# Score matmuls of the exact attentions on 64 rows a head, two heads abreast

## The chip, the cores and the metric

One core of one Trainium2 chip. The time is that of one execution on the device in microseconds (us); a kernel's time is the median of its runs. A core has five engines with a queue each: TensorE (PE; its weight loads are listed apart as PEld), VectorE (DVE), ScalarE (ACT), GpSimd (POOL), and SyncE (SP), which here only issues DMAs. Each works through its own list of instructions in order, and they meet at semaphores.

## What is computed

The reference passes x, four sequences of 512 tokens by 128 features, through four layers that also read a context of 154 tokens a sequence:

- L0: cross attention with 16 heads of 8 features and a padding mask, added to x, layer norm
- L1: causal self attention, cross attention, a mixture of 8 experts (the best 2 for each token), each with a layer norm
- L2: self and cross attention with values rounded to 8 bits, and a gated feed-forward
- L3: grouped cross attention with 16 query heads of 64 features, and a gated feed-forward

The change touches the three attentions of L0 and L1 that are computed exactly:

```
scores = einsum('bqhd,bkhd->bhqk', q, k) / sqrt(8)   # + padding or causal mask
attn   = softmax(scores, axis=-1)
out    = einsum('bhqk,bkhd->bqhd', attn, v)
```

## The kernel before

Work is cut into units, one attention (or other stage) of one sequence. Units 0 to 3 are L0, 4 to 7 the causal self attention (SELF), 8 to 11 the cross attention of L1 (CROSS); these twelve are the exact units. Later stages are the experts, the 8-bit attentions, a feed-forward, the grouped attention and the last feed-forward.

**Operands.** Queries and keys are each split into three bf16 terms, whose products are summed for nearly fp32 scores. `Q_TERMS` and `K_TERMS` name eight pairs of terms, so a head of 8 features becomes a stack of 64 rows. Two heads, a pair, lie one above the other in the 128 rows of `q_stack`. The keys lie in `k_half` (`k_half_ctx` for a context), once for each head of the pair, with zeros in the 64 rows of the other head. So each score matmul runs over all 128 rows and gives one head. The stacks are made by DMA: SP writes the terms to device memory (L806) and reads them back in 16 pieces for the keys (L788) and 16 for the queries (L795).

**Scores, first way round (`scores_exact`).** A step takes one pair of heads and, in a cross unit, two query tiles of 128, in SELF one query tile n with its 128(n+1) keys. A cross unit has 16 steps, a SELF unit 32. The two heads go to the two halves (PSUM banks) of `score[at_step % 2]`. L0 adds the padding row with a second matmul for each; SELF adds the causal mask by a matmul with the identity (`ident_bf`, `causal`). DVE then takes the maximum over the keys (L1927). Two steps can be in flight.

**Scores, second way round (`scores_transposed`).** A block has keys on the 128 partitions and up to 512 queries as columns, in one bank of `trans`. Keys times queries (L1124), in SELF the mask (L1126), then minus the maxima through a matmul with `ones` (L1128). ACT takes the exponential of the whole bank (L1483). A group of 4 heads has 5 blocks in a cross unit (one a head, and a tail for the keys past 128, L1116 and L1118, which runs over all 128 rows) and 10 in SELF, with one or two pieces each. The 320 blocks of all units are the slots: PE's order is, for each slot w, block w; then the score steps that `place_steps` spreads evenly over the slots (those of the next group of heads, the first of them 3 slots ahead); then the items of `EXACT_ITEMS` (projections K, Q and V, normaliser N1 and N2, output projection W, transpositions H and "tops", and others); then, if a batch of blocks is complete, their weighing of the values (`weigh_batch`, L1149, L1151), which works on 32 columns of the array a head, four heads at a time.

```
for w in range(EXACT_SLOTS):
    scores_transposed(w)
    for u, i in steps_in_slot(w):
        scores_exact(u, i)
    for it in EXACT_ITEMS.get(w, ()):
        item(*it)
    if weigh_in_slot(w) is not None:
        weigh_batch(weigh_in_slot(w))
```

Block w waits until the exponential of block w-2 is done. The keys and queries of the next unit are projected in slots 0 and 1 of a cross unit (1 and 2 in SELF); its first score step is in slot 13 of 20, or 28 of 40, and waits for its stacks. `split_tops` on DVE splits the maxima of a group in three bf16 terms, in columns 32j to 32j+2 for head j of the group.

## Time and profile before

| | |
|---|---|
| median of 3 runs | 1636.1 us (1633.66 to 1645.17) |
| the profiled execution | 1633.61 us, span 1631.8 us |
| busy in the span | PE 1165.1, PE's weight loads 676.5, DVE 1109.7, ACT 903.4, POOL 677.9 us |
| mean granted clock of TensorE | 0.825 |

The span runs from the first to the last instruction; start and end of the program lie around it (1.8 us). Busy times are sums over stages with different limits. Matmuls are pipelined, so a matmul's own duration is longer than the time from its start to the next start. The granted clock has two levels, 1.00 (2.4 GHz) and 0.50 (1.2 GHz); a value between is a mean over time.

### The profile page before, as it was taken

The page shows a single profiled execution, that of the slowest core. Times are in us where ns is not written, and L with a number is a line of the kernel's source. Part 1 is how long each engine was busy: PE and PEld are TensorE (multiplying, and loading weights), DVE is VectorE, ACT ScalarE, POOL GpSimd, SP SyncE. Part 2 cuts the span into 40 slices and gives each one's busy share as a digit, 9 for nine tenths or more (in the row PEclk, how much of TensorE's full clock was granted, in tenths as well). Part 3 has the DMA queues.
Part 4 walks back from the last instruction along what each step waited for, and adds up shares of the span by engine and source line. Part 5 has one row for each costly group of instructions (what it writes and reads, how often), then busy time and mean ns, then how long its engine had stood idle before and what let it go on. Part 6 is the DMA issues. An engine that isn't in the chain of part 4 may idle for free.

```text
span 1631.8 us, 27753 instructions
## 1 busy us (share of the span) xinstructions
PE 1165.1 (71%) x8832; PEld 676.5 (41%) x8832; DVE 1109.7 (68%) x3127; ACT 903.4 (55%) x2546; POOL 677.9 (42%) x1048
## 2 busy tenths in 40 slices
PE   2689999999978789684435354444438778888888
PEld 1355555555544448682111111122215444553545
DVE  2466776777667756277989899977764666666533
ACT  0344455555544346347767778888882254545542
POOL 5201110110111142545888878877771245344320
PEclk9899999999989999896555555555558899999999
DMA  5322341121072211216645557665560112111000
GB/s 160 69 49 55 64 139 36 43 73 35 17 150 48 46 45 46 80 46 162 120 95 111 100 108 123 119 106 107 106 108 10 26 38 55 28 33 48 1 1 26
DMA packets 263825, 115.53 MB, mean 71 GB/s; under 512 B 215928, under 2 KB 252672, under 8 KB 261504
## 3 DMA queue, kind: packets, MB, share of 16 engines
q1 hardware_dynamic: 258720, 107.34, 31.2%
q0 software_dynamic: 2048, 4.20, 0.9%
q10 hardware_dynamic: 2912, 2.22, 0.5%
q8 instruction: 71, 1.16, 0.3%
q14 instruction: 74, 0.61, 0.1%
HBM read 38.54 MB, written 16.45 MB: 34 GB/s over the span
## 4 chain that ended last, share of the span: by engine, by line
PE 39%; POOL 19%; DVE 15%; issue 15%; ACT 8%; DMA 2%; SPq 1%; another core or an unknown queue 0%; POOLq 0%; ACTq 0%; DVEq 0%
POOL arena L2236 10%; ACT arena L1536 5%; PE acc L1151 3%; PE trans L1124 3%; PE trans L1128 3%; POOL inv_total L2225 2%; PE misc L988 2%; PE misc L994 2%; PE score L1098 2%; PE trans L1275 2%; PE score L1090 2%; DVE minus_top L1927 2%; POOL arena L2183 2%; PE score L1287 2%; PE score L1289 2%
## 5 line engine op out<-in xcount | busy, mean ns | idle before, releaser
L2236 POOL TENSOR_SCALAR arena<-arena,inv_total 128x512 f16<-128x512 f32 (+1 forms) x512 | 299.6, 585 | 57.3 <-DVE inv_total L2003 16.4
L1927 DVE TENSOR_REDUCE minus_top<-score 128x4 f32<-128x616 f32 (+4 forms) x256 | 204.2, 804 | 150.9 <-PE score L1094 61.2
L2099 POOL TENSOR_TENSOR rstd<-spread,minus_half 128x4 f32<-128x4 f32 x36 | 37.6, 1044 | 534.0 <-DVE spread L1617 464.6
L1536 ACT ACTIVATE arena<-score,minus_top,exp_scale 128x512 f32<-128x512 f32 (+1 forms) x340 | 210.4, 625 | 17.5 <-POOL arena L2236 7.5
L1483 ACT ACTIVATE arena<-trans 128x512 f32<-128x512 f32 x240 | 140.5, 597 | 119.1 <-PE trans L1128 113.3
L1574 ACT ACTIVATE arena<-arena,minus_top 128x154 f32<-128x154 f32 x256 | 105.1, 412 | 131.8 <-DVE minus_top L2068 131.7
L1232 PE MATMUL score<-arena 32*128 32x512 bf16 (+1 forms) x340 | 68.4, 455 | 144.2 <-ACT arena L1536 143.1
L2009 DVE TENSOR_REDUCE top_score<-score 128x2 f32<-128x1024 f32 (+1 forms) x128 | 135.7, 1060 | 0.6 <-PE score L1232 0.5
L2256 POOL TENSOR_TENSOR arena<-arena,inv_total 128x512 f32<-128x512 f32 x64 | 66.5, 1040 | 144.7 <-DVE inv_total L2076 130.9
L1128 PE MATMUL trans<-arena 128*128 128x512 bf16 (+3 forms) x384 | 123.3, 330 | 0.0
L1536 ACT ACTIVATE arena<-trans,minus_top,exp_scale 128x154 f32<-128x154 f32 (+1 forms) x172 | 105.5, 620 | 16.3 <-POOL arena L2236 11.7
L1090 PE MATMUL score<-arena 128*128 128x154 bf16 x512 | 74.2, 244 | 51.9 <-issue 45.8
L2063 DVE CUSTOM_DVE_ANT_0 arena<-score,arena 128x154 f32<-128x154 f32 x256 | 66.0, 314 | 60.1 <-PE score L1312 59.7
L1992 DVE TENSOR_SCALAR arena<-arena 128x1024 bf16<-128x1024 f16 x192 | 102.7, 535 | 6.0 <-DMA arena<-arena 6.0
L1232 PEld LDWEIGHTS score<-arena 32*128 32x128 bf16 x340 | 14.2, 102 | 195.1 <-ACT arena L1536 177.8
L1527 ACT ACTIVATE minus_top<-top_score,exp_scale 128x2 f32<-128x2 f32 (+1 forms) x192 | 56.4, 294 | 60.9 <-DVE top_score L2009 60.4
L1232 PE MATMUL trans<-arena 32*128 32x154 bf16 (+1 forms) x172 | 34.4, 448 | 73.3 <-ACT arena L1536 73.2
L1090 PEld LDWEIGHTS score<-arena 128*128 128x128 bf16 x512 | 49.0, 104 | 79.7 <-issue 52.4
L1151 PE MATMUL acc<-arena 128*32 128x512 f32 (+3 forms) x768 | 78.5, 496 | 2.7 <-ACT arena L1483 2.7
L1501 ACT ACTIVATE arena<-score,arena 128x128 f32<-128x128 f32 x184 | 51.9, 371 | 49.8 <-PE score L1188 42.4
L1251 PE MATMUL acc<-arena 128*32 128x128 bf16 x1536 | 58.6, 304 | 28.1 <-DVE oT L2017 15.5
L1124 PE MATMUL trans<-arena,late 128*128 128x512 bf16 (+3 forms) x256 | 77.3, 302 | 0.2 <-ACT arena L1483 0.2
(283 smaller groups left out, 3075.7 us busy)
## 6 DMA issues: line engine op xcount, KB each, us to landing
arena<-q_terms SPq DMA_DIRECT2D x176, 64.0 KB
late<-arena SPq DMA_DIRECT2D x128, 64.0 KB, 2.0
q_terms<-arena SPq DMA_DIRECT2D x36, 128.0 KB
late<-k_terms SPq DMA_DIRECT2D x64, 64.0 KB
arena<-arena SPq DMA_TRANSPOSE x192, 3.1
by_expert<-zeros SPq DMA_DIRECT2D x2, 1472.0 KB, 9.8
arena<-by_expert SPq DMA_DIRECT2D x10, 256.0 KB, 2.9
from_expert<-arena SPq DMA_DIRECT2D x10, 256.0 KB
```

Of the source, the lines that this page charges most:

```text
L1090: ins = nc.tensor.matmul(dst, q_stack[:, u % 2, c, t * P:(t + 1) * P], k_half_ctx[:, u % 2, s, c, 0:CTX], start=True, stop=(stage(u) != L0))
L1124: nc.tensor.matmul(dst, keys, q_stack[:, u % 2, h // 2, q0:TOKENS], start=True, stop=False)
L1128: ins = nc.tensor.matmul(dst, ones[:, j, :], top_rows[:, g % 2, q0:TOKENS], start=False, stop=True)
L1151: ins = nc.tensor.matmul(acc[32 * j:32 * j + 32, q0:TOKENS], v_cols[:, k, 4 * g + j, :], src, start=(b % half == 0 and k == 0), stop=(last ...
L1232: ins = nc.tensor.matmul(quant_score[i % 3][:, j, z * n:(z + 1) * n], qT_codes[r:r + 32, u % 2, t * P:(t + 1) * P], k4_codes[r:r + 32, u % ...
L1483: nc.scalar.activation(expT[w % SLOTS], trans[w % 2][:, :], ACT.Exp, bias=bias)\
L1536: ins = nc.scalar.activation(probs[:, i % 3, j, of], quant_score[i % 3][:, j, of], ACT.Exp, bias=minus_top[:, at_col:at_col + 1], scale=ex ...
L1574: ins = nc.scalar.activation(gq_exp_p[:, i % 3, h, :], shifted[:, i % 3, h, :], ACT.Exp, bias=minus_top[:, at_col:at_col + 1], accum_out=t ...
L1927: nc.vector.tensor_reduce(dst, src, axis=AX.X, op=ALU.max, negate=True).then_inc(top_ready, 1)
L1992: nc.vector.tensor_scalar(pT_codes[:, of, :, :].rearrange("p k q -> p (k q)"), pT_raised[:, of, :, :].rearrange("p k q -> p (k q)"), -HALF ...
L2009: nc.vector.tensor_reduce(of_step(top_score, i), src, axis=AX.X, op=ALU.max, negate=True).then_inc(quant_top, 1)
L2236: ins = nc.gpsimd.tensor_scalar(codes[:, (i - 1) % CODE_SOURCES, j, to], probs[:, (i - 1) % 3, j, of], inv_total[:, at_col:at_col + 1], HA ...
```

## The change

A head's score matmuls use only its own 64 rows: head s of a pair takes rows 64s to 64s+63 of `q_stack` and of a single `k_stack` without zeros. The two heads' matmuls are issued one behind the other and go to two banks. The same holds for the blocks: blocks w and w+1 are raised together, piece by piece, at the even slots; a cross unit's tail stays alone and on 128 rows. For the pairs to hold one head of either half, the last SELF blocks of a group take heads (0, 2) and (1, 3) instead of (0, 1) and (2, 3), and the maxima of head j go to row block 2(j % 2) + j // 2. Masks on 64 rows need the identity and the mask in two halves, so the causal addition becomes two matmuls a head. The constants for this (`masks`) come with the late loads and are converted on DVE in slot 14 of unit 1 (`mk`). The padding row's three terms go to rows 0 to 2 of either half, for which POOL multiplies with `term_row` and adds. The clearing of `k_half` and `k_half_ctx` on POOL is gone. The steps' places are as before.

```diff
+def transposed_with(w):
+    u, g = BLOCKS[w][:2]
+    n = (w - FIRST_SLOT[u]) % PER[u]
+    if n % 2:
+        return []
+    return [w, w + 1] if n + 1 < PER[u] else [w]
...
-    at(exact, 0, ("zk", 0))
+    at(exact, FIRST_SLOT[1] + 14, ("mk", 0))
...
-                     (causal_f, io["causal"]), (causalT_f, io["causalT"]), (head_mask[:, :], io["head_mask"]),
+                     (head_mask[:, :], io["head_mask"]), (term_row[:, :], io["term_row"]),
...
-                    for s in range(2):
-                        bank = score[at_step % 2][:, s, :]
-                        if is_cross(u):
-                            for j in range(2):
-                                t = 2 * n + j
-                                dst = bank[:, j * CTX:(j + 1) * CTX]
-                                ins = nc.tensor.matmul(dst, q_stack[:, u % 2, c, t * P:(t + 1) * P],
-                                                       k_half_ctx[:, u % 2, s, c, 0:CTX], start=True,
-                                                       stop=(stage(u) != L0))
...
+                    banks = [(half_rows(s), score[at_step % 2][:, s, :]) for s in range(2)]
+                    if is_cross(u):
+                        for j in range(2):
+                            t, of = 2 * n + j, slice(j * CTX, (j + 1) * CTX)
+                            for r, bank in banks:
+                                ins = nc.tensor.matmul(bank[:, of], q_stack[r, u % 2, c, t * P:(t + 1) * P],
+                                                       k_stack_ctx[r, u % 2, c, 0:CTX], start=True, stop=(stage(u) != L0))
+                            if stage(u) == L0:
+                                for r, bank in banks:
+                                    ins = nc.tensor.matmul(bank[:, of], ones_pad[r, :], pad_rows[r, u % 2, :],
                                                            start=False, stop=True)
+                    else:
+                        width = P * (n + 1)
+                        for r, bank in banks:
+                            nc.tensor.matmul(bank[:, 0:width], q_stack[r, u % 2, c, n * P:(n + 1) * P],
+                                             k_stack[r, u % 2, c, 0:width], start=True, stop=False)
+                        for h in range(2):
+                            for r, bank in banks:
+                                ins = nc.tensor.matmul(bank[:, width - P:width], unit_halves[r, h, :], causal[r, h, :],
+                                                       start=False, stop=(h == 1))
                     ins.then_inc(scores_ready, 1)

                 def scores_transposed(w):
+                    blocks = transposed_with(w)
+                    if not blocks:
+                        return
                     u, g, _, pieces = BLOCKS[w]
                     if w >= 2:
-                        pe.wait_ge(expT_ready, w - 1)
+                        pe.wait_ge(expT_ready, blocks[-1] - 1)
...
+                    for n in range(len(pieces)):
+                        _, k, q0, c0 = pieces[n]
+                        two = [(j, half_rows(j % 2), 2 * g + j // 2, trans[z % 2][:, c0:c0 + TOKENS - q0])
+                               for z in blocks for j in [BLOCKS[z][3][n][0]]]
+                        for j, r, c, to in two:
+                            keys = (k_stack_ctx if is_cross(u) else k_stack)[r, u % 2, c, k * P:(k + 1) * P]
+                            nc.tensor.matmul(to, keys, q_stack[r, u % 2, c, q0:TOKENS], start=True, stop=False)
                         if is_causal(u):
+                            for h in range(2):
+                                for j, r, c, to in two:
+                                    nc.tensor.matmul(to[:, 0:P], unit_halves[r, h, :], causalT[r, h, :], start=False, stop=False)
+                        for j, r, c, to in two:
+                            ins = nc.tensor.matmul(to, ones[r, j, :], top_rows[r, g % 2, q0:TOKENS], start=False, stop=True)
+                    ins.then_inc(scoresT_ready, 2)
...
+                    elif name == "mk":
+                        dve.wait_ge(late_in, 16 * LATE_LOADS)
+
+                        for h in range(2):
+                            r = slice(h * P // 2, (h + 1) * P // 2)
+                            nc.vector.tensor_scalar(before_bf[r, :], masks_f[r, 1, h, :], 0.0, None, ALU.is_lt)
+                        nc.vector.tensor_copy(masks[:, :, :, :], masks_f).then_inc(masks_ready, 1)
```

## Rows read from the trace of the kernel before

**Rows 1.** The page's 40 slices of 40.8 us: busy tenths of PE, granted clock.

```profile
PE   2689999999978789684435354444438778888888
...
PEclk9899999999989999896555555555558899999999
```

**Rows 2.** Windows by unit (2, 5, 9, 11): stretch, length, busy time of each engine, clock.

```profile
134.20:172.50 38.30, 35.66 (x262) 19.99 (x260) 28.12 (x69) 20.30 (x34) 4.64 (x7) 1.00 0.37 75
...
271.10:329.00 57.90, 55.17 (x500) 31.88 (x499) 42.83 (x90) 30.71 (x53) 4.25 (x4) 1.00 0.17 51
...
484.20:524.70 40.50, 32.62 (x203) 17.25 (x201) 28.64 (x92) 18.07 (x35) 4.61 (x7) 0.92 0.26 49
...
566.20:602.10 35.90, 28.21 (x166) 13.01 (x163) 24.61 (x87) 15.61 (x29) 19.28 (x19) 1.00 0.14 45
```

**Rows 3.** Timeline of PE at three first score steps: start, duration, work, idle time before.

```profile
122.72 0.23 PE L1090 MATMUL score<-arena 128*128 128x154 bf16 x1 [2.28 <-issue]
...
162.67 0.23 PE L1090 MATMUL score<-arena 128*128 128x154 bf16 x1 [1.05 <-issue]
...
513.31 0.42 PE L1090 MATMUL score<-arena 128*128 128x154 bf16 x2 [5.96 <-issue]
```

**Rows 4.** Timeline of SP's DMA issues in unit 9.

```profile
489.88 1.80 SPq L806 DMA_DIRECT2D q_terms<-arena  x3
...
498.05 5.37 SPq L795 DMA_DIRECT2D arena<-q_terms  x16
```

**Rows 5.** Timeline of PE around a weighing (128x128, then 128x32, then 128x128).

```profile
206.47 0.22 PE L1098 MATMUL score<-late,arena 128*128 128x128 bf16 x1
206.52 0.22 PE L1100 MATMUL score<-causal,ident_bf 128*128 128x128 bf16 x1
206.67 1.06 PE L1151 MATMUL acc<-arena 128*32 128x512 f32 x8
207.67 1.12 PE L1149 MATMUL acc<-arena 128*128 128x512 f32 x2
208.63 0.38 PE L1124 MATMUL trans<-arena 128*128 128x512 bf16 x1
208.84 0.38 PE L1128 MATMUL trans<-arena 128*128 128x512 bf16 x1
```

**Rows 6.** Timeline of PE in the grouped attention; fp32 matmuls have two records each.

```profile
1423.40 0.79 PE L1312 MATMUL score<-arena 64*128 64x154 f32 x8
1424.13 0.65 PE L1323 MATMUL trans<-ident,arena 128*128 128x128 f32 x4
```

**Rows 7.** Timeline of ACT in unit 5: two exponentials back to back.

```profile
308.43 1.09 ACT L1483 ACTIVATE arena<-trans 128x512 f32<-128x512 f32 x2
```

**Rows 8.** Windows of parts of units 0, 2, 5 and 9, columns as in rows 2.

```profile
46.50:52.10 5.60, 5.60 (x37) 4.75 (x38) 2.40 (x3) 0.97 (x2) 0.00 (x0) 0.50 0.10 33
...
134.20:139.70 5.50, 5.43 (x36) 2.66 (x34) 5.02 (x15) 3.18 (x6) 0.00 (x0) 1.00 0.11 25
163.70:172.50 8.80, 8.80 (x78) 5.49 (x77) 5.43 (x11) 5.74 (x10) 3.61 (x6) 1.00 0.40 66
...
271.10:290.70 19.60, 18.36 (x139) 9.87 (x138) 15.43 (x31) 9.88 (x18) 0.00 (x0) 1.00 0.34 97
290.70:305.90 15.20, 13.72 (x132) 8.42 (x131) 12.62 (x36) 7.45 (x13) 4.25 (x4) 1.00 0.20 68
305.90:317.50 11.60, 11.60 (x119) 6.85 (x118) 7.39 (x12) 7.02 (x13) 0.00 (x0) 1.00 0.01 1
...
513.30:516.30 3.00, 2.99 (x17) 2.17 (x18) 0.86 (x2) 1.16 (x2) 0.00 (x0) 0.50 0.00 0
...
513.30:524.70 11.40, 10.60 (x73) 6.63 (x74) 8.01 (x38) 5.42 (x11) 0.00 (x0) 0.87 0.00 0
```

**Rows 9.** Timeline of DVE in the first block: the wait for the first loads.

```profile
11.41 0.23 DVE L759 CAST ident_bf<-ident 128x128 bf16<-128x128 f32 x1 [6.98 <-DMA attn_w<-in_attn_w]
```

**Rows 10.** Timeline of POOL: the clearing of `k_half`.

```profile
32.48 6.92 POOL L2150 MEMSET late<- 128x8192 f32 x1
```

More of the change, by code:

```diff
@@ L100, in exact_batches @@
             out.append((g, [[(j, 1, P, 0), (j, 3, 3 * P, 3 * P)] for j in range(4)]))
-            out.append((g, [[(j, 2, 2 * P, 0), (j + 1, 2, 2 * P, 2 * P)] for j in (0, 2)]))
+            out.append((g, [[(j, 2, 2 * P, 0), (j + 2, 2, 2 * P, 2 * P)] for j in (0, 1)]))
     return out
@@ L395, in build @@
         ident_bf = sb("ident_bf", [P, P], bf16)
-        causalT = sb("causalT", [P, P], bf16)
-        causal = sb("causal", [P, P], bf16)
+        masks = sb("masks", [P, 3, 2, P], bf16)
+        unit_halves, causal, causalT = (masks[:, n, :, :] for n in range(3))
         q_bias = sb("q_bias", [P, 2])
         head_mask = sb("head_mask", [P, 4])
+        term_row = sb("term_row", [P, 3])
         expert_no = sb("expert_no", [P, EXPERT_BLOCKS])
@@ L1130, in scores_transposed @@
-                    ins.then_inc(scoresT_ready, 1)
+                    if len(blocks) == 1:
+                        bank = trans[w % 2]
+                        pe.wait_ge(k_tail_ready, seq(u) + 1 + (B if stage(u) == CROSS else 0))
+                        for z in range(2):
+                            nc.tensor.matmul(bank[:, :], k_tail[:, u % 2, g, z * P:(z + 1) * P],
+                                             q_stack[:, u % 2, 2 * g + z, :], start=(z == 0), stop=False)
+                        nc.tensor.matmul(bank[:, :], ones_tail, top_rows[:, g % 2, :], start=False, stop=True)\
+                            .then_inc(scoresT_ready, 1)
+                        return
```

98 lines of the change are left out of this document (37 added, 61 removed).

## The prediction

> **What bounds the kernel now.** The page's slices come first: up to slice 15 (some 600 us) PE is busy in 8 or 9 tenths and its clock is nearly full; from slice 18 to 29 the clock is at its lower level and PE is not what matters [rows 1]. All edits lie before 602 us, so only the twelve exact units count. I cut them at the start of each unit's first exponential (ACT's 320 exponentials are the 320 blocks, in order). The windows by unit [rows 2] show three kinds: an L0 unit takes 38.3 us with PE busy 35.7; a SELF unit 57.9 with PE 55.2, DVE 42.8; a CROSS unit 40.5 with PE only 32.6, DVE 28.6. CROSS has fewer matmuls than L0 and is no shorter, so PE can't be its whole bound. The waits of PE tell why: at the first score step of the next unit PE stands still 2.28, 1.05 and 5.96 us [rows 3] (a third L0 wait is 2.2, two further CROSS waits 7.5 and 4.2, unit 0 has 10.1). These are waits for that unit's query and key stacks: SP issued the query terms at 489.88, the last sixteen reads until 503.4, and PE goes on at 513.31 [rows 3, 4], 23.4 us after the first issue; in the L0 units it is 22.3. That trip is DMA, and the change issues as many DMAs of the same size. So a cross unit is a chain: slots 0 and 1 up to the query projection, the trip, then slots 13 to 19. What PE saves between the projection and slot 13 only lengthens the wait. SELF units show no such wait: their trip has 28 slots to hide in.
>
> **The price of a matmul.** From start to start in the timeline 512 columns take 0.21 to 0.22 us and 128 take 0.05 to 0.06 [rows 5]; I use 0.216 and 0.056, and 0.067 for 154, which is 0.42 ns a column and 2.5 ns for each matmul.
>
> **Two heads abreast (removed work).** No bf16 pair on 64 rows is in this trace. The nearest row is the fp32 score step of the grouped attention, the same form (64 rows each, two banks): eight records of 154 columns in 0.79 us, the next operation 0.73 after its start [rows 6]. One after another they would need 8 x 0.128 = 1.03 and a switch; two abreast 4 x 0.13 = 0.52, and 0.2 for the switch and the first weights: 0.73. So I take full overlap. Per L0 unit: 16 steps of eight matmuls become four pairs, -0.27 each, -4.3; 16 head blocks of two 512-column matmuls, -0.216 each, -3.5; sum -7.8. CROSS has no padding matmuls: -2.1 - 3.5 = -5.6. SELF: the score columns, 8 x 1280, are halved, -4.3; the causal additions double in number and go two abreast, 0; the blocks have 4 x 10,240 key and top columns, halved, -8.5; sum -12.8.
>
> **Switches of the array (added work).** Between matmuls of different row or column shape PE loses time: the 128-column matmul at 206.52 should hand over at 206.58, the 32-column ones begin at 206.67, 0.095 more; the 128x128 fp32 one at 207.67 takes 0.96 to the next start where two passes of 0.427 are 0.85, so 0.106 of weight load is exposed; bf16 weights expose about 0.01 [rows 5]. Now only the weighing of values switches: 8 times in a cross unit, 26 in SELF. Walking the slot table with the new order (64-row stretches broken by every projection, transposition of tops, normaliser, tail and weighing) gives about 33 in L0, 34 in CROSS, 47 in SELF: +3.3, +3.5 and +3.0 us. PE's own work changes by -4.5, -2.1 and -9.8 a unit, -67 us over twelve units (19 + 39 + 9). That is the most that can be won.
>
> **Blocks raised in pairs (a new wait).** The pair (w, w+1) may be raised only when the exponentials of all blocks before w are done; now block w needs only w-2. Behind the waiting PE stand the score steps, so DVE waits too. One cycle: raise 0.55 or 0.66 (1280 or 1536 columns a pair of blocks), 0.16 until the last columns are out, 0.04 to ACT, two exponentials 1.09 [rows 7], 0.05 back: 1.9 to 2.0 us. In slots 20 to 39 of a SELF unit nothing but blocks, steps and weighing runs, 11.6 us for 10 slots, PE without a gap, DVE 7.4 [rows 8]. Its five pairs will hold 1.7, 0.9, 2.0, 0.9 and 2.7 us of PE work (the raise, one or two steps of 0.17 to 0.33, in three of them a weighing of 0.5 to 0.95 and its switches), 8.2 in sum; with a floor of 1.95 each it is 10.5, and 10.8 with part of the present surplus (11.6 measured, 10.4 counted). Gain 0.8 for each of two groups, 1.6, where PE alone would give 6. In slots 0 to 19 (34.8 us, PE 32.1, DVE 28.05 [rows 8]) PE falls by 6.0 to 26.1, two short pairs give 2.3 back, 28.4; DVE is now level with it. With the present surplus of 2.7 and a little for two engines of equal load, 31.6: gain 3.2. SELF: 4.8 a unit, 19 for four. Bounds: 0 (every pair adds a stall that the surplus doesn't hold) to 9.8 (ACT runs in the shadow).
>
> **Cross units.** Slots 0 and 1 of an L0 unit: PE 5.4, DVE 5.0 of 5.5 [rows 8]; at most 0.4. Slots 13 to 19: 2.1 less PE work out of 8.8 [rows 8], some 0.5 back in the pair after each single tail, which must await the tail's exponential (N1, N2 and H stand behind three of the four tails and hide them). Gain 1.5 each. But the wait of 1.05 grows to some 3; after the waits of 2.3 the granted clock is at its lower level for 4 us, after the one of 1.05 it is not; after the CROSS wait it is 0.50 for 513.3 to 516.3 [rows 8]. One more cold stretch costs 1.5. Units 1 to 3: 3 us. CROSS 8 to 10: 0.2 + 1.1 - 0.7 = 0.5 each, DVE already 8.0 of 11.4 there [rows 8]; unit 11, which has no successor to wait for but a router chain on DVE, 1. Sum 2.5. The first scores and slots 0 and 1 of unit 0 run largely at the lower clock [rows 8], where a step of eight matmuls costs 8 x 0.128 = 1.03 and DVE's reduction of it 0.8: six to eight such steps on the path, 2 us, and slots 13 to 19, 1.5.
>
> **Edits with small prices.** The first block now loads six things instead of seven before DVE's last preparations, which wait for them [rows 9], and three DVE conversions go: an issue and a landing of 0.4 to 0.5 and 3 x 0.14, -0.9 (0.7 with what the new mask preparation takes, below). The memset of 6.9 us on POOL goes [rows 10], and nobody waited for it; POOL's padding work gains some 1.2 us a sequence, POOL being idle most of a unit. The new mask preparation (three DVE instructions, 1.1 us by the elements of the casts beside it) stands in unit 1, slot 14, just behind the wait for DMA: 0 to +1, I take 0.2. Splitting the tops keeps its four small instructions. Late loads grow by 0.4 MB; their first reader is POOL, 20 us ahead of need: 0.
>
> **The sum**: 0.7 + 3.5 + 3 + 19 + 2.5 = 28.7 us. The profiled execution took 1633.6 (span 1631.8), so 1605; the median of the three runs is 2.5 above it, so **1607**.
>
> **Rivals.** (a) *PE's saving counts in full*: ACT's cycle falls into the gaps, DVE keeps up. For: in SELF, ACT is busy only 30.7 of 57.9 [rows 2]. Against: the order of instructions ties raise and exponentials, whatever the mean. SELF 9 each, the rest 15: 1636 - 51 = 1585, at best 1569. (b) *Narrow pairs don't overlap*: two weight loads of 128 columns may not go in 0.056 us; the fp32 pair has 0.13 for them [rows 6]. Then each 128-column pair costs 0.112. A SELF unit has some 150 of them (64 in the steps, 64 in the blocks, the rest narrow keys), +8.5 us of PE work: SELF gains 0 to 1, 1636 - 10 = 1626. (c) *Slower, by the clock*: PE would stand still about 1 us in three pairs of five. If the lower level were granted in slots 20 to 39 of SELF, 8.2 us of work in 10 slots become 16.4 against 11.6 now: +9.6 a unit, 38 for four, and with the other gains of 22 the kernel takes 1652; it decides from about two thirds of those stretches upward. Against: the last CROSS unit kept 1.00 with PE busy 28.2 of 35.9 [rows 2]. (d) *The change doesn't do what it says*: pairs go one after another. SELF then adds 6.8 of causal columns and 3.0 of switches, the cross units 1 each: 1636 + 47 = 1683. It turns to a loss in SELF once a pair costs 1.5 single streams (19.6 x 1.5 + 3 = 32.4).
>
> By the Trainium skill, "TensorE: Matmul & The Clock Gate", section "Measured speedup vs the span model", four row tiles gave 3.07 times, not four; two tiles with that loss would cost 1.3 streams, SELF's work would fall by 3.9 rather than 9.8, and the result would lie at (b). The trace's pair [rows 6] shows no such loss. The same page, "A second HAM failure mode: psum-queue depth-cycling", says that short idle stretches between groups of matmuls can keep pulling the clock down, which is (c); no row here shows it for gaps of 1 us.
>
> **Chances.** Forecast 0.60, (a) 0.14, (b) 0.16, (c) 0.06, (d) 0.04. The range leaves out (c), (d) and the best of (a): 1578 to 1627. 1% (16 us) is about what a measurement can tell from no change: faster 0.75 (forecast, (a), a third of (b)), same 0.16, slower 0.09.
>
> **What will show it.** Pairs: starts of the new score matmuls a few ns apart and 0.216 us from pair to pair at 512 columns; PE work in SELF near 46 a unit. The cycle: in slots 20 to 39 PE idle ahead of the raised pairs, released by ACT, 10.5 to 11 us for 10 slots. The trip: waits before the first score step longer by about 2 us, 22 to 23 us from issue to use as before. Clock 1.00 through SELF. I am wrong if SELF stays at 57 or goes under 50, or if the cross units shrink by more than 3.

## The result, and the profile after

| | before | after |
|---|---|---|
| median of the runs measured together | 1645.01 us (18 runs, 1629.49 to 1653.57) | 1634.83 us (18 runs, 1617.46 to 1646.02) |
| ratio | | 0.9931, 95% interval 0.9903 to 0.996 |
| profiled execution, span | 1633.61, 1631.8 us | 1629.24, 1627.4 us |
| first exponential, start of unit 4, of unit 8, end of unit 11 | 42.9, 212.1, 442.6, 602.1 | 40.0, 206.0, 429.1, 594.2 |
| PE, PE's weight loads, DVE, ACT busy | 1165.1, 676.5, 1109.7, 903.4 | 1109.7, 600.2, 1109.3, 895.0 |

The ratio is of the means of the fast runs, 16 of the 18 after, and not of the two medians. Faster by 0.4 to 1.0%, some 11 us, where 29 was forecast. In the profiled executions the exact units gain 7.9: the start 2.9, units 0 to 3 went from 169.2 to 166.0, SELF from 230.5 to 223.1, and CROSS got longer, from 159.5 to 165.1. What follows unit 11 took 1024 to 1043 us in all the executions told of here, whatever the kernel, so below it is also told where unit 11 ends. That is one execution each: units 1 to 3 alone differ by up to 5.4 us between executions of the same code.

Two of the page's slice lines of after, to be held against [rows 1]:

```profile
PE   2688888787777679784435354444439787898888
...
PEclk9899999999998999796555555555559889999999
```

Up to slice 15 PE has gone from mostly 8 and 9 tenths to 7 and 8; the clock is as uneven as it was. Windows of units 2, 5, 9 and 11, as in [rows 2]:

```profile
125.60:166.40 40.80, 33.35 (x266) 14.33 (x262) 28.06 (x68) 19.76 (x34) 4.66 (x7) 0.92 0.40 80
263.20:318.90 55.70, 44.84 (x630) 23.94 (x628) 42.16 (x90) 29.35 (x53) 4.25 (x4) 1.00 0.16 53
470.40:512.70 42.30, 31.29 (x204) 12.73 (x200) 29.25 (x92) 18.18 (x36) 4.62 (x7) 0.91 0.27 50
556.40:594.20 37.80, 26.84 (x162) 9.90 (x160) 23.97 (x83) 15.45 (x29) 19.34 (x19) 0.95 0.14 43
```

In SELF PE has lost 10.3 us of work (55.17 to 44.84) and the unit 2.2 (57.9 to 55.7). Units 2 and 9 are longer with less work, at a clock of 0.92 and 0.91 that was 1.00 and 0.92. Now SELF's ten-slot stretches (slots 0 to 9, 10 to 19, 20 to 29) and the stretch of unit 9 behind the wait, as in [rows 8]:

```profile
263.20:282.80 19.60, 16.17 (x172) 7.76 (x170) 15.54 (x31) 9.52 (x17) 0.00 (x0) 1.00 0.36 115
282.80:297.30 14.50, 11.15 (x168) 6.54 (x166) 12.34 (x35) 7.22 (x14) 4.25 (x4) 1.00 0.13 46
297.30:308.10 10.80, 8.76 (x152) 4.82 (x150) 7.13 (x12) 6.59 (x13) 0.00 (x0) 1.00 0.01 2
...
499.73:512.70 12.97, 11.34 (x76) 5.15 (x76) 8.81 (x39) 5.57 (x12) 0.00 (x0) 0.76 0.00 0
```

Slots 20 to 29 are what was forecast, 10.8. Slots 0 to 9 take 19.6 as before, with PE's 18.4 down to 16.2. The stretch of unit 9 behind the wait went from 11.4 to 13.0, at a clock of 0.76 that was 0.87. PE's timeline where a pair of blocks is raised (start, duration, work):

```profile
270.52 0.34 PE L1149 MATMUL trans<-arena,late 64*128 64x384 bf16 x2
270.69 0.28 PE L1153 MATMUL trans<-masks 64*128 64x128 bf16 x4
270.80 0.33 PE L1155 MATMUL trans<-arena 64*128 64x384 bf16 x2
270.97 0.22 PE L1149 MATMUL trans<-arena,late 64*128 64x128 bf16 x2
```

Two matmuls of 384 columns take 0.17 from start to next start, four of 128 take 0.11: one after another they would take 0.33 and 0.22 (by the prediction's 0.42 ns a column and 2.5 ns for each matmul). Both kinds run fully abreast. The next timeline is cut from one of all engines, around the end of one pair and the start of the next, in slots 20 to 29:

```profile
296.85 0.38 PE L1155 MATMUL trans<-arena 64*128 64x512 bf16 x2
...
297.27 1.08 ACT L1509 ACTIVATE arena<-trans 128x512 f32<-128x512 f32 x2 [1.00 <-PE trans L1155]
...
297.71 0.64 PE L1177 MATMUL acc<-arena 128*32 128x256 f32 x8
298.40 0.10 PEld L1149 LDWEIGHTS trans<-arena,late 64*128 64x128 bf16 x2 [0.54 <-ACT arena L1509]
298.41 0.39 PE L1149 MATMUL trans<-arena,late 64*128 64x512 bf16 x2
```

ACT waits 1.00 for PE to finish the pair, then PE waits for both exponentials: the two take turns. PE's first score steps of units 2, 3 and 10 (to [rows 3]) and SP's issues in unit 9 (to [rows 4]):

```profile
114.20 0.31 PE L1106 MATMUL score<-arena 64*128 64x154 bf16 x2 [3.91 <-issue]
...
154.85 0.31 PE L1106 MATMUL score<-arena 64*128 64x154 bf16 x2 [3.68 <-issue]
...
499.73 0.44 PE L1106 MATMUL score<-arena 64*128 64x154 bf16 x4 [6.70 <-issue]
```

```profile
476.10 1.80 SPq L818 DMA_DIRECT2D q_terms<-arena  x3
...
483.95 5.33 SPq L807 DMA_DIRECT2D arena<-q_terms  x16
```

From 476.10 to 499.73 are 23.6 us: the trip is what it was (23.4), and the waits are longer (2.28, 1.05 and 5.96 before).

### The profile page after: what moved, and what is told of

The parts are those of the page before. It is cut to its first block, busy times and chain, and to the rows that moved or that the text cites. A ratio compares the mean times of both kernels' runs of the same rounds, so it can differ in the third digit from the quotient of the medians.

```text
span 1627.4 us, 28786 instructions
## 1 busy us (share of the span) xinstructions
PE 1109.7 (68%) x9344; PEld 600.2 (37%) x9344; DVE 1109.3 (68%) x3126; ACT 895.0 (55%) x2546; POOL 681.6 (42%) x1054
## 3 DMA queue, kind: packets, MB, share of 16 engines
q1 hardware_dynamic: 258720, 107.61, 31.6%
q0 software_dynamic: 2048, 4.20, 0.9%
## 4 chain that ended last, share of the span: by engine, by line
PE 35%; POOL 19%; issue 17%; DVE 15%; ACT 10%; DMA 2%; SPq 1%; POOLq 0%; another core or an unknown queue 0%; ACTq 0%; DVEq 0%
POOL arena L2268 10%; ACT arena L1562 5%; PE acc L1177 3%; PE trans L1149 2%; POOL inv_total L2257 2%; PE misc L999 2%; PE misc L1005 2%; PE trans L1301 2%; ACT arena L1509 2%; POOL arena L2215 2%; PE score L1313 2%; PE score L1315 2%; PE trans L1155 2%; PE acc L1175 1%; DVE arena L1727 1%
## 5 line engine op out<-in xcount | busy, mean ns | idle before, releaser
L1509 ACT ACTIVATE arena<-trans 128x512 f32<-128x512 f32 x240 | 134.5, 596 | 113.8 <-PE trans L1155 107.8
L1562 ACT ACTIVATE arena<-trans,minus_top,exp_scale 128x154 f32<-128x154 f32 (+1 forms) x172 | 105.6, 621 | 16.2 <-POOL arena L2268 11.8
L1106 PE MATMUL score<-arena 64*128 64x154 bf16 x512 | 45.7, 248 | 54.0 <-issue 32.7
L1509 ACT ACTIVATE arena<-trans,arena 128x512 f32<-128x512 f32 x80 | 52.3, 687 | 30.6 <-PE trans L1155 27.0
L2044 DVE TENSOR_REDUCE top_score<-trans 128x2 f32<-128x1024 f32 (+1 forms) x64 | 67.4, 1053 | 0.0
L1447 ACT COPY arena<-misc 128x512 bf16<-128x512 bf16 x48 | 28.1, 586 | 70.1 <-PE misc L989 67.3
```

The lines of the kernel that those rows point to most:

```text
L1509: nc.scalar.activation(expT[w % SLOTS], trans[w % 2][:, :], ACT.Exp, bias=bias)\
L1562: ins = nc.scalar.activation(probs[:, i % 3, j, of], quant_score[i % 3][:, j, of], ACT.Exp, bias=minus_top[:, at_col:at_col + 1], scale=ex ...
L2044: nc.vector.tensor_reduce(of_step(top_score, i), src, axis=AX.X, op=ALU.max, negate=True).then_inc(quant_top, 1)
```

## The experiments

Kernels that were measured together share their runs of the kernel before; each ratio is to those. "Ends at" is the end of unit 11 in the profiled execution (before 602.1, after 594.2). The changed kernel's own ratio, 0.9931, is from other runs than those of the experiments.

### 1. The clock behind the waits

Filler matmuls (their results are overwritten) ahead of the wait for the stacks, in the changed kernel and in the one before:

```
+ if i == 0 and u in FILL:
+     pe.wait_ge(top_ready, at_step - 1)
+     for _ in range(FILL[u]):   # after {1:24, 2:14, 3:14, 4:10, 9:28, 10:26, 11:16}, before {1:36, 2:8, 3:3, 4:8, 9:28, 10:22, 11:15}
+         nc.tensor.matmul(score[at_step % 2][:, 0, :], ident_bf[:, :], q_stack[:, (u - 1) % 2, 0, :], start=True, stop=True)
```

> The changed kernel, with filler matmuls of 512 columns (10 to 28 of them, 2 to 6 us) ahead of PE's wait for the stacks of the next cross unit, into the score bank that the next step overwrites; they change no value. Theory A (the clock): in the changed kernel the granted clock is 0.50 for 68.5 us before the end of the exact units, against 51.2 before, nearly all of it right behind these waits, which costs some 10 us. Expected: the cold stretches behind the waits go (under 30 us in all), units 1 to 3 about 1.5 and units 8 to 11 about 2 us shorter each, the kernel 8 to 12 us below the changed one (ratio to before 0.985 to 0.988). Rival B (the clock costs nothing there, since the trip of the stacks or DVE sets the end of each unit): units as long as before within 0.5, ratio 0.993 as for the changed kernel.

> Control: the kernel before, with the same filler (3 to 36 matmuls of 512 columns) in front of the same waits. Theory A: its cold stretches behind the waits are 21.6 us in all against some 43 in the changed one, so it gains about half, 3 to 6 us (ratio 0.996 to 0.998), and the distance between this and the changed kernel with filler is larger than the 11 us between the two without: 14 to 18. Rival B: ratio 1.00.

After with filler: 0.9932 (0.9903 to 0.996), ends at 589.4, clock at 0.50 for 34 us instead of 68. Before with filler: 0.9987 (0.9955 to 1.002), ends at 594.2, 14 us at 0.50. Unit 2 of the one and of the other:

```profile
124.70:162.40 37.70, 33.92 (x276) 14.37 (x272) 28.05 (x68) 19.59 (x33) 4.66 (x7) 1.00 0.38 82
```

```profile
131.50:170.40 38.90, 36.31 (x265) 20.29 (x264) 28.22 (x69) 20.28 (x34) 4.65 (x7) 1.00 0.37 75
```

Units 1 to 3 took 113.6 with filler against 120.8 without; in the kernel before 115.8 against 117.9. So in L0 the clock is where the gain went, as far as one execution each can tell, and 2.2 of the 3 us forecast appear once it is held. In CROSS the changed kernel got nothing back: 167.0 against 165.1. But there the filler didn't hold the clock: waits of 3.8 and 3.6 us were left at two trips, and 24 of the 34 us at 0.50 lie in these units (31 without filler). Where it was held better, CROSS did get shorter: in the kernel before from 159.5 to 154.6, with 3 us at 0.50 instead of 24. So this run doesn't clear the clock in CROSS.

The expectations were missed: both ratios are above theirs, and the two kernels with filler are 6.6 us apart in the median and 4.8 in where unit 11 ends, not 14 to 18. The filler is worth 5 us in the changed kernel (1623.3 against 1628.5 of the kernel with serial steps below, which does the changed kernel's work and was measured together with it; with 95% confidence that difference is known to some 4.5 us), not 8 to 12. The clock took a part of the gain, and not most of it.

### 2. One block at a time; one head after the other

First the old raising (block w after the exponential of w-2), each block on 64 rows; then the changed kernel with all of one head's score matmuls of a step before the other's.

```
- pe.wait_ge(expT_ready, blocks[-1] - 1)
+ pe.wait_ge(expT_ready, w - 1)          # and the pieces of block w alone
```
```
- for j in range(2): for r, bank in banks: ...     # and the same for keys and masks in SELF
+ for r, bank in banks: for j in range(2): ...
```

> The changed kernel with blocks raised one at a time again, each on its head's 64 rows, with the old wait (block w waits for the exponential of w-2); the score steps stay two heads abreast. PE's work in SELF goes up by 8.5 (key and top columns) and 3.6 (64 more causal additions of 0.056) a unit, to some 55. Theory A (DVE and the order of work bound slots 0 to 19, ACT's cycle slots 20 to 39, and pairing the blocks is what took 0.8 per ten slots): SELF units back at 57 to 59 us, slots 20 to 39 at 11.6 or more per ten slots, cross units 0 to 1 longer than in the changed kernel, ratio to before 0.997 to 1.003. Rival C (the pair's wait for the older exponential is what ate the gain): SELF units at or below the changed kernel's 55.8, slots 0 to 19 shorter than 34.1, ratio below 0.993.

> The changed kernel with the score matmuls of one head behind those of the other (still 64 rows each); the blocks stay in pairs. In SELF PE does 4.3 us more of score columns and 3.6 us more of causal additions a unit (some 53 in all against 45), in cross units 2 to 4 more. Theory A: in slots 0 to 19 of SELF, where DVE is the fuller engine (27.8 of 34.1), PE goes from 27.3 to some 31 and the stretch gets 1 to 2 us longer; slots 20 to 39 stay at 10.8 to 11.2 per ten, since ACT's cycle sets them: SELF 57 to 58. Cross units +0 to +1 (the trip covers most). Ratio 0.997 to 1.002. If PE's work counted in full, SELF would be 63 and the ratio 1.02.

Single blocks: 0.9995 (0.9963 to 1.0028), ends at 595.2, SELF 57.0. Slots 0 to 9 and 20 to 29 of unit 5:

```profile
262.60:282.30 19.70, 18.71 (x171) 9.80 (x167) 15.55 (x31) 9.87 (x18) 0.00 (x0) 1.00 0.36 83
...
297.40:308.50 11.10, 10.63 (x154) 6.60 (x152) 7.30 (x12) 6.96 (x13) 0.00 (x0) 1.00 0.01 3
```

With 2.5 us more of PE work slots 0 to 9 are 0.1 longer (19.7); slots 20 to 29 take 0.3 more (11.1 where 11.6 or more was expected). Pairing the blocks is worth 1.3 us a SELF unit (57.0 to 55.7) for 8.5 us of work saved.

The serial steps were meant to add 8 us of work to a SELF unit and added none (0.9962, 0.9931 to 0.9993; ends at 593.8). Its timeline, and slots 0 to 9 of unit 6:

```profile
284.04 0.27 PE L1113 MATMUL score<-late,arena 64*128 64x256 bf16 x2
284.15 0.28 PE L1116 MATMUL score<-masks 64*128 64x128 bf16 x4
```

```profile
318.90:338.50 19.60, 16.19 (x172) 7.79 (x170) 15.55 (x31) 9.52 (x17) 0.00 (x0) 1.00 0.35 108
```

The program has the second head's key matmul fourth, and it starts with the first one's: each half of the rows works through its own matmuls. (The trace tells starts; that the queue holds them in the program's order is taken from the program.) So this run settles nothing on PE's work, but it is the changed kernel once more, measured together with the others.

### 3. Which engine holds SELF

Half the exponential in SELF (256 of a block's 512 columns); and the normaliser's four reciprocals on 4 of 128 columns, in the changed kernel and in the one before.

```
+ of = slice(0, TOKENS if is_cross(u) else TOKENS // 2)
  nc.scalar.activation(expT[w % SLOTS][:, of], trans[w % 2][:, of], ACT.Exp, bias=bias)
```
```
- nc.vector.reciprocal(inv_sum[:, of], inv_sum[:, of])
+ nc.vector.reciprocal(inv_sum[:, n * P:n * P + 4], inv_sum[:, n * P:n * P + 4])
```

> The changed kernel, but in SELF units ACT takes the exponential of 256 of a block's 512 columns only (the other half of the block keeps old numbers). Two exponentials then take some 0.65 us and not 1.09. Theory A (in slots 20 to 39 the cycle raise, first exponential, second exponential, next raise is the bound, PE idle 1 us in it): ten slots fall from 10.8 to 8.8 to 9.2, where PE's own 8.8 takes over; slots 0 to 9 fall by less than 1 (they are bound by the chain of projections, V's spreading on DVE and the weighing). SELF units 50 to 52, the kernel 16 to 22 us less than the changed one (ratio 0.980 to 0.985). Rival D (PE's switches and weight loads are what is left, ACT runs in their shadow): ten slots stay above 10.4, ratio 0.992.

> The changed kernel with the four reciprocals of the normaliser on 4 columns and not on 128 (the rest isn't inverted): 4 times some 0.8 us less work on DVE in slots 5 to 8 of each unit. Theory A (in slots 0 to 19 of SELF DVE's queue sets the pace since PE got 2.1 to 2.6 us lighter per ten slots): slots 0 to 9 go from 19.6 to 17 to 18.5, SELF 54 or less, ratio 0.985 to 0.989. Rival E (DVE isn't on the path; the pair's wait and the single misc buffer are): 19.6 stays within 0.4, ratio 0.993.

> Control: the kernel before with the same short reciprocals. Theory A (PE, busy 18.3 of 19.6 in slots 0 to 9, is the bound before): slots 0 to 9 fall by 0 to 0.8, SELF by under 1, ratio 0.998 to 1.000. If it falls as far as in the changed kernel, DVE's queue was the bound in both, and PE's saving in these slots was never to be had.

Half exponentials: 0.9894 (0.9851 to 0.9937), SELF unit 5 at 55.0 where 50 to 52 was expected, slots 0 to 9 at 19.2. Slots 10 to 19 and 20 to 29 of unit 5:

```profile
285.10:301.30 16.20, 12.80 (x168) 6.97 (x166) 12.67 (x36) 5.09 (x14) 4.26 (x4) 0.89 0.27 72
301.30:311.10 9.80, 8.68 (x152) 4.81 (x150) 7.04 (x12) 4.44 (x12) 0.00 (x0) 1.00 0.01 3
```

With 2.2 us less of ACT work ten slots fall by 1.0, not by 2: the cycle raise, exponentials, raise is the bound there, but something else in it doesn't shrink with ACT's work; which part is not shown. In slots 10 to 19 of every SELF unit the clock fell to 0.50 for 3.4 us, which cost 1.7 (14.5 to 16.2): rival (c) of the forecast, in small.

Short reciprocals: 0.9937 (0.9904 to 0.997) after, 0.9984 (0.9946 to 1.0022) before. Slots 0 to 9, after and before:

```profile
264.10:283.70 19.60, 16.18 (x174) 7.76 (x170) 12.75 (x31) 9.52 (x18) 0.00 (x0) 1.00 0.36 105
```

```profile
267.80:287.40 19.60, 18.15 (x137) 9.88 (x138) 12.93 (x31) 9.90 (x18) 0.00 (x0) 1.00 0.34 97
```

2.5 to 2.8 us less on DVE change nothing. Theory A's word on slots 0 to 9, that DVE sets them, fell here. PE 16.2 to 18.7, DVE 12.8 to 15.5: 19.6 or 19.7 in all of them. PE's waits in that stretch of the changed kernel (total, times, longest; a fourth is 0.2) say what is left, a chain:

```profile
PE misc L999 <- ACT arena L1435: 1.0, 1, 1.0
PE trans L1149 <- ACT arena L1509: 1.0, 1, 1.0
PE acc L1177 <- issue: 1.0, 1, 1.0
```

N1 waits for ACT to empty `misc` of Q, the weighing waits for V's spreading on DVE (it ends at 273.84 in the timeline, the weighing starts at 273.94), a pair waits for the exponentials before it.

### 4. The chain in SELF

SELF's items set apart, in either kernel:

```
- V 4, Q 2, N1 3, r 5 6 7 8, N2 9, W 10, M 12, H 14, cna 14, cnb 15, cnc 17
+ V 3, Q 5, N1 7, r 9 11 12 13, N2 15, W 17, M 21, H 24, cna 24, cnb 26, cnc 29
```

> The short reciprocals showed that DVE's load is not what holds slots 0 to 9 of SELF at 19.6 us: DVE fell from 15.5 to 12.8 and nothing moved, as it doesn't move with PE's 16.2 or 18.7. New theory G: these slots are a chain of items through the one misc bank (K at slot 1, Q at 2, N1 at 3, V at 4, N2 at 9, W at 10), each of which PE can only raise after ACT or DVE has emptied the last, with the pair's wait in between. This kernel is the changed one with SELF's items set apart (V 3, Q 5, N1 7, reciprocals 9, 11, 12 and 13, N2 15, W 17, M 21, H 24). Expected by G: slots 0 to 9 fall from 19.6 to 16.5 to 17.5, slots 10 to 19 rise from 14.5 to no more than 15, slots 20 to 29 from 10.8 to about 11.5, since what moves falls into PE's gaps: SELF 53 to 54.5, the kernel 6 to 11 us below the changed one (ratio 0.986 to 0.990). Rival H (each slot pays its own waits wherever the items stand): SELF 55.5 to 57, ratio 0.993.

> Control: the kernel before with the same places of the items. PE is busy 55.2 of 57.9 there, 2.7 us of gaps a unit, so by G at most 1.5 to 2.5 us a SELF unit can be won, 4 to 8 us in all (ratio 0.995 to 0.998), less than in the changed kernel, whose gaps are 11 us a unit. If it gains as much as the changed kernel, the places of the items held both alike.

After 0.9909 (0.9877 to 0.994), ends at 576.0, SELF 52.8; before 0.9919 (0.9889 to 0.995), ends at 587.8, SELF 54.5 (unit 6). Slots 0 to 9 and 20 to 29 of unit 6 after, then all four tens of it before:

```profile
312.70:327.70 15.00, 14.00 (x168) 7.08 (x166) 11.56 (x27) 9.52 (x17) 0.00 (x0) 1.00 0.20 62
...
341.30:354.70 13.40, 10.37 (x158) 5.70 (x160) 10.57 (x26) 7.77 (x15) 3.25 (x3) 1.00 0.04 13
```

```profile
319.60:336.10 16.50, 16.16 (x134) 9.10 (x133) 12.05 (x27) 9.85 (x17) 0.00 (x0) 1.00 0.21 62
336.10:350.30 14.20, 14.20 (x130) 8.41 (x129) 12.11 (x27) 6.43 (x12) 1.01 (x1) 1.00 0.39 136
350.30:362.60 12.30, 12.30 (x125) 7.53 (x124) 10.45 (x26) 8.05 (x15) 3.25 (x3) 1.00 0.01 1
362.60:374.10 11.50, 11.50 (x118) 6.74 (x117) 7.38 (x12) 6.38 (x11) 0.00 (x0) 1.00 0.00 0
```

The stretch fell further than expected (15.0), and slots 20 to 29, where the moved items went, rose further (13.4). Shown is that the places of the items alone are worth 3 us a unit, at the same work; which link of the chain it was, the bank `misc` or the spreading on DVE, is read from the three waits and was not tested singly. The places held both kernels alike (2.9 and 3.4 us a unit, where 1.5 to 2.5 was expected before), so the chain explains why slots 0 to 9 didn't move, and not where the rest went. With it gone the kernel before is PE-bound (54.2 of 54.5), and the changed one, with 9.2 us less to do, is 1.7 faster: 2.1 in slots 0 to 19, where the change alone had brought 0.7, 0.7 in the last ten, and a loss of 1.1 in slots 20 to 29, 13.4 against 12.3. In the medians the two are only 2.7 us apart, a difference known to some 7 us; by where unit 11 ends it is 11.8.

### 5. The pair's wait alone

The kernel before with the items set apart, blocks on 128 rows one after another, but with the pair's wait and one signal for both:

```
- pe.wait_ge(expT_ready, w - 1);  block w;  .then_inc(scoresT_ready, 1)
+ pe.wait_ge(expT_ready, w);      blocks w and w + 1;  .then_inc(scoresT_ready, 2)
```

> The kernel before with SELF's items set apart (54.5 us a SELF unit, PE busy 54.2), and blocks raised in pairs with the pair's wait and one signal at the end of the pair, but all on 128 rows, one after another: PE's work as before, only the wait is new. If the wait costs what I forecast (the stall of about 1.25 us a pair in place of double buffering, only partly covered): slots 20 to 39 from 11.6 to 12.8 to 13.5 per ten, SELF 58 to 62, the kernel 14 to 30 us above the 1616 of the one with single blocks. If double buffering was worth nothing: within 3 us.

1.009 (1.0058 to 1.0123), median 1654.1, ends at 620.6, SELF 60.3. The four tens of unit 6, to be held against the last four rows above:

```profile
339.80:356.30 16.50, 16.23 (x134) 9.12 (x132) 11.97 (x27) 9.52 (x17) 0.00 (x0) 1.00 0.22 65
356.30:371.60 15.30, 14.45 (x130) 8.38 (x128) 12.29 (x27) 6.02 (x11) 1.01 (x1) 1.00 0.53 108
371.60:386.40 14.80, 12.73 (x124) 7.49 (x122) 9.75 (x26) 7.77 (x14) 3.25 (x3) 1.00 0.08 17
386.40:400.10 13.70, 11.90 (x119) 6.89 (x118) 7.14 (x12) 6.03 (x12) 0.00 (x0) 1.00 0.00 0
```

PE is busy 55.3 and the unit takes 60.3 instead of 54.5. The wait costs 5.8 us a SELF unit, 1.1 in slots 0 to 19 and 4.7 in slots 20 to 39; on the kernel it is about 1.7%, L0 included (units 0 to 3 took 174.5 against 168.1). With the rows halved nearly the same order of work takes 52.8: running two abreast saves 7.5, and 1.7 is left. A pair fills both banks of `trans`, so no block can be raised while ACT reads. The Trainium skill, "Perfetto Trace Analysis", section "Optimizing Tensor Performance", says that independent matmul groups should rotate through different banks so that emptying one overlaps the next group; by that rule the change gives up what the rule buys, and the price measured here agrees.

### 6. The cross units

Key reads issued by ACT, so that the query reads go out earlier; the expert weights behind unit 9's stacks; and the next unit's K and Q projected in slots 16 and 17 of the unit before:

```
+ if u + 1 in {1, 2, 3, 9, 10, 11} and 4 <= n < 9: read_keys_by_act(u + 1, ...)    # on ACT, 3 or 4 of the 16 a slot
```
```
  if u == 9:
+     sp.wait_ge(q_stacked, 32 * len(Q_TERMS) * (u + 1))
      sp.dma_start(e_all[:, :, 0:FF], ...)
```
```
- at(exact, f + (0 if u else 2), ("K", nxt)); at(exact, f + (1 if u else 3), ("Q", nxt))
+ at(exact, f - 4, ("K", nxt)); at(exact, f - 3, ("Q", nxt))     # units 2, 3, 9, 10, 11, and Q of 4
```

> The changed kernel, with the 16 reads of the next cross unit's keys (units 1 to 3, 9 to 11) issued from ACT's queue in slots 4 to 8, so that SP can issue the query reads 5 us earlier; that adds 16 issues of some 0.32 us to ACT. Theory A (these units are gated by the trip of the stacks, PE waiting 3 to 7 us ahead of the first score step): the waits shrink by 3 to 5 us, units 9 to 11 get 3 to 4 us shorter, units 1 to 3 2 to 3, with the clock's drops behind the waits going too: 12 to 20 us in all, ratio 0.981 to 0.986. Rival F (the bytes, not the issues, set the trip; or ACT's issues delay the exponentials as much): under 4 us, ratio 0.991 to 0.994.

> The changed kernel, where SP waits until unit 9's query stacks have landed before it issues the 2.3 MB of expert weights, which now go out right behind the query reads of unit 9 and share the DMA engines with them (busy 9 tenths there, the trip 25.7 us against 22.6 to 23.6 in the other cross units). Theory I (the trip is set by the bytes in flight): unit 9's trip falls to 22 to 23, PE's wait in unit 8 from 7.3 to about 4, unit 8 by 3 us, the others as they were: ratio 0.990 to 0.992. Rival: the weights collide with unit 10's reads in place of unit 9's and nothing is won, 0.993.

> The changed kernel with the earlier projections alone. By the trip: SELF as in the changed kernel (55.7), cross units 1 to 3 and 8 to 10 shorter by 3 to 6 each, 18 to 30 us in all, ratio 0.976 to 0.983. If another chain of the cross units (normaliser, output projection, layer norm, DVE busy 29 of 42) stands right behind the trip: 5 to 10 us.

Reads by ACT: 0.9934 (0.9901 to 0.9967), ends at 590.1. The query reads left 4.1 us behind the first write of the terms instead of 7.9. From that write to PE's first score step the trips took 18 to 26 us all the same (18 to 26 in the changed kernel too, 22.1 and 22.4 in the mean of seven), though the one in unit 9 was shorter, 20.1. In unit 9:

```profile
478.70 5.67 SPq L808 DMA_DIRECT2D arena<-q_terms  x16
```

```profile
494.71 0.44 PE L1107 MATMUL score<-arena 64*128 64x154 bf16 x4 [3.15 <-DMA arena<-k_terms_ctx]
```

The releaser is now a key read. The ratio is rival F's: the issuing doesn't set the trip. That the bytes in flight do is what the next run speaks for; this one doesn't tell it from a longer wait for the keys. The Trainium skill, "DMA: Bandwidth & Descriptors", section "Issuing engines are not separate DMA queues", says that DMAs issued by different engines run on the same 16 DMA engines, and that a second issuer saves only the time to issue them; this run agrees.

Late weights: 0.9915 (0.9887 to 0.9943), ends at 592.0. The wait in unit 8, after (first row) and here:

```profile
460.50 0.44 PE L1106 MATMUL score<-arena 64*128 64x154 bf16 x4 [7.31 <-issue]
```

```profile
461.70 0.44 PE L1106 MATMUL score<-arena 64*128 64x154 bf16 x4 [4.32 <-issue]
```

The trip fell from 25.7 to 22.7, the unit from 41.4 to 38.1, as expected; in eight other executions of changed kernels with the weights there that trip took 24.6 to 26.7. The prediction had not reckoned with that collision; it is in both kernels. The weights are 4 MB (one DMA of 2048 KB and eight of 256), not the 2.3 of the expectation. The ratio alone (0.9931 without the edit) would not show it.

Earlier projections: 0.9858 (0.9825 to 0.9892), 1618.8, ends at 583.2. Units 1 to 3 took 109.5 (120.8), but unit 0, where two of the projections went, 53.1 (45.2): together 162.6 against 166.0. Unit 8 took 37.8 and unit 10 36.5 (41.4 and 43.7), CROSS in all 156.4 (165.1), with waits left in units 8 and 9. The 18 to 30 us expected were missed: unit 11 ends 11.0 earlier. So the trip is a bound of the CROSS units, and something else stands close behind it.

### 7. All together, and the change's own worth

> The changed kernel with all that helped or should help: filler matmuls ahead of the waits for the stacks, SELF's items set apart, the expert weights behind the stacks of unit 9. If the three add up: 5 from the clock, 6 to 11 from the items, 3 from the weights, 14 to 19 us below the changed kernel, ratio 0.981 to 0.985; 0.986 to 0.990 if G is wrong.

> The changed kernel with both chains opened: SELF's items set apart as before; the queries and keys of the next cross unit (2, 3, 9, 10, 11, and the queries of unit 4) are projected four slots before the unit that they are projected in now (slots 16 and 17 of the unit before), so the stacks land about 6 us earlier against the blocks; expert weights behind unit 9's stacks. No filler. If the trip is what holds the cross units: units 1 to 3 at 34 to 36, units 8 to 10 at 35 to 38, PE's waits ahead of the first score step under 1 us, cold stretches under 30 us before the end of unit 11. SELF 52.8. The exact units shorter by 13 (SELF) and 25 to 35 (the rest): the kernel at ratio 0.968 to 0.977. If the trip was no bound: 0.988.

> Control: the kernel before with the same three moves. If both chains hid the change's worth, this kernel stays PE-bound (SELF 54.5, L0 units at PE's 35.5 to 37, CROSS at 34 to 38) and ends 12 to 22 us above the other, ratio 0.982 to 0.987. If it comes within 5 us of the other, the change isn't worth more than that in any case.

> The changed kernel, items of SELF set apart, projections of the next cross unit four slots earlier, expert weights issued once unit 11's stacks have landed, 28 filler matmuls ahead of unit 1's stacks. Units 1 to 3 36 each, SELF 53, units 8 to 10 33 to 38 each and no cold stretch after unit 0 except a few us: the exact units end at 545 to 558 us (594 in the changed kernel), ratio 0.970 to 0.976.

> The kernel before with the same moves (36 fillers). PE-bound in SELF at 54.5 and in the L0 units at 37 to 39: the exact units end 12 to 20 us later than in the other, at 562 to 575, ratio 0.980 to 0.985. If the change is worth nothing of its own, the two end within 5 us of each other.

| kernel | ratio to before | median | unit 11 ends at |
|---|---|---|---|
| after: filler, items apart, late weights | 0.9826 (0.9798 to 0.9853) | 1605.0 | 563.0 |
| after: items apart, early projections, late weights | 0.9805 (0.9771 to 0.9839) | 1606.2 | 566.2 |
| before: the same | 0.9805 (0.9769 to 0.9841) | 1609.0 | 579.9 |
| after: as above, weights behind unit 11's stacks, 28 fillers ahead of unit 1's | 0.9774 (0.9728 to 0.9819) | 1593.1 | 557.9 |
| before: the same, 36 fillers | 0.9834 (0.9791 to 0.9877) | 1602.6 | 565.0 |

The first row met its expectation; the second missed it (0.968 to 0.977), the third too: it is 2.8 us above the second in the median, where 12 to 22 was expected, and within the 5 us that were to mean that the change isn't worth more. In the second and third row the weights, issued on SP's queue around the start of unit 9, held up unit 10's trip in both (unit 9 took 48.1 and 46.1); the last two rows have them moved. The fourth missed its ratio (0.970 to 0.976), the fifth met it (0.980 to 0.985). Units 0 to 3, SELF and CROSS of the last two kernels, after and before:

```profile
39.30:201.60 162.30, 130.44 (x1062) 57.08 (x1078) 109.91 (x248) 76.10 (x129) 33.34 (x57) 0.96 0.29 59
201.60:412.40 210.80, 180.14 (x2470) 94.66 (x2466) 159.88 (x362) 118.97 (x219) 18.14 (x20) 1.00 0.23 67
412.40:557.90 145.50, 112.77 (x748) 44.60 (x759) 107.01 (x334) 67.14 (x127) 33.24 (x40) 0.94 0.34 79
```

```profile
42.30:202.80 160.50, 145.83 (x1041) 83.05 (x1060) 108.06 (x245) 78.47 (x128) 26.99 (x51) 0.98 0.28 58
202.80:424.00 221.20, 213.15 (x1953) 126.80 (x1983) 165.85 (x363) 124.41 (x219) 18.12 (x20) 1.00 0.25 63
424.00:565.00 141.00, 121.38 (x747) 61.72 (x758) 106.75 (x334) 67.72 (x127) 33.24 (x40) 0.96 0.32 81
```

The fourth kernel beats both given ones. The last two differ by 9.5 us in the median, known to some 7 us, and by 7.1 in where unit 11 ends; with the trips and the items out of the way the change is worth no more than it was with them in, and all of it is in SELF and the start. It removes 33 us of PE work from SELF here and shortens it by 10, of which 2.6 are a single stall in the other kernel's unit 4. I had expected 12 to 20 between them. Over six pairs of kernels that differ by the change alone (the given ones, with filler, with short reciprocals, with the items apart, and the two pairs here) the medians differ by 2.7 to 12.3 us. So the two chains did not hide the change. In SELF the pair's wait paid most of it away.

## Why the prediction was right or wrong

The forecast was 1607 of 1636.1, a ratio of 0.982; measured were 0.9931 and 1634.8. The profiled execution gains 7.9 us up to the end of unit 11 where 28.7 were forecast: SELF fell short by 11.6, CROSS by 8.1, units 1 to 3 by 5.9, and the start and unit 0 gave 4.8 more than forecast. By its number rival (b) comes nearest (1626; 0.9931 of 1636.1 is 1625), which is chance: its mechanism isn't there.

- **Pairs run abreast; PE's work.** Right. SELF's work fell by 10.3 (forecast 9.8), narrow pairs included. Rivals (b), narrow pairs one after another, and (d), all pairs so, fell with the timeline of a raised pair. The loss that the Trainium skill gives for four row tiles ("TensorE: Matmul & The Clock Gate", "Measured speedup vs the span model") does not show with two. The split was off: 6.0 less was booked in slots 0 to 19 and 4.8 came (32.1 to 27.3).
- **Slots 20 to 39.** Right: 10.8 per ten, gain 1.5 a unit (forecast 1.6), PE idle behind ACT.
- **Slots 0 to 19, "34.8 to 31.6: gain 3.2".** This is the step that failed. Measured 34.1, gain 0.7. I had added PE's reduced work, 2.3 for short pairs and a surplus, as if PE set the time. Slots 0 to 9 were not bound by PE: [rows 8] show 18.36 of 19.60 and I took the gap for slack, where a chain of items held the stretch at 19.6. Nor was DVE "level with it": with 2.8 us less of DVE nothing moved. Four times 2.5 are 10 of SELF's 11.6.
- **The pair's wait.** Named as the new wait, and well priced: 4.4 in slots 20 to 39 (6.0 of saving there against a gain of 1.6) and 2.3 in slots 0 to 19, 6.7 in all. The run with the wait alone gives 4.7 and 1.1, 5.8. What failed in slots 0 to 19 is not this price but the bound under it.
- **Units 1 to 3, gain 3.** Measured -2.9 in the profiled executions; in five other executions with these units as in the changed kernel 115.3 to 119.0 for the three, in three of the old ones 116.8 to 117.9: no difference. The text priced "one more cold stretch" at 1.5; there were 68 us at 0.50 instead of 51 up to unit 11, and holding the clock brought 2.2 of the 3 back.
- **CROSS, gain 2.5.** Measured -5.6; over the executions with these units untouched (160 to 165 in five of the new ones, 159.5 to 161.2 in three of the old) some -3. The trips took 25.7, 23.6 and 22.6 (25.0, 23.4 and 21.7 before), a little over the 22 to 23 forecast. Slots 2 to 9 of units 9 and 10, where I had booked nothing but also no loss, take 13.0 against 12.7 and 12.9 with 0.8 less PE work; with the wait alone they take 13.5, so there too a pair's wait eats the overlap. The clock was at 0.50 for 31 us of these units, before for 24. With the trips earlier and the weights moved the changed CROSS units are still no shorter (145.5 against 141.0). Why they are 4 longer there is open: part may be clock (0.94 against 0.96).
- **Start and unit 0, 0.7 and 3.5.** Measured 2.9 and 6.1; over the executions about 2 and 3. The unit is right, the start was priced too low.
- **The clock as a rival (c).** SELF kept 1.00 but for 3.4 us in unit 6. With ACT halved it fell in each unit, in slots 10 to 19. The mechanism exists; the place was mostly the cross units.

## What to carry to other kernels

Before booking an engine's saving, show that the stretch follows that engine: 18.4 busy of 19.6 looked like a bound and was not (19.6 with PE's work at 16.2 too). Running two heads abreast doubles PE's rate only if the results have somewhere to go: with as many banks as the pair fills, its gain is paid back as turns between producer and reader (here 7.5 won, 5.8 lost). Look at the trips and at the places of small items first: those moves, with filler ahead of unit 1's stacks, brought the old kernel 28 us (1630.7 to 1602.6) and the new one some 26 (0.9931 to 0.9774 of the same 1630.7), more than the change did in any pair.

## What was not expected of the hardware

Matmuls on the two halves of the rows need not stand alternately in the program: with six in it head by head, the second head's first one still started 3 ns behind the first head's, and PE's work was 16.19 against 16.17 us in ten slots. A lighter PE was granted a lower clock more often: up to the end of unit 11 it was at 0.50 for 51, 44 and 44 us in three executions of the kernel before or near it, for 68 to 75 in six of the changed one or near it (51 with the projections earlier), 82 with ACT halved, 34 (changed) and 14 (before) with filler. And 4 MB of weights behind a trip's reads lengthened it by 3 us.
